# Rotary pieces of q and k kept in PSUM, in an attention and mixture-of-experts block on one core

## Chip, cores and metric

One core of one Trainium2 chip runs the whole kernel as one program. The metric is the time on the device in microseconds (us), the median over runs. A profiled execution of the same program gives the trace.

## The reference

The layer takes x of 16 batches x 1024 tokens x 256 channels in fp32. The part that matters here is how q and k are made:

```python
h  = _layernorm(x) * (1 + ca) + sa                 # modulation, one row per batch
xn = (h - mu) * rsqrt(var + eps) * gamma + beta    # second norm
q, k, v = heads(xn @ Wq + bq), heads(xn @ Wk + bk), heads(xn @ Wv + bv)   # 16 heads of 16
rot = stack([x1 * cos - x2 * sin, x1 * sin + x2 * cos])   # q and k; x1, x2: even and odd channels
```

After it come causal softmax attention, the output projection with residuals, and eight experts with gather and scatter-add.

## The kernel before

`build` runs five phases, each a block of five engine programs with a barrier between blocks. The change touches `phase1` alone. It makes q, k and v for all 16 batches and stores them to HBM; `phase2` (attention) reads them back.

**Pieces.** The q or k projection of 512 tokens is one piece. A batch has four (two blocks of 512 tokens, q and k), so there are 64 pieces, n = 0 to 63. A piece is two halves of 128 partitions x 512 columns: the even channels (e = 0) and the odd ones (e = 1) of all heads.

**Slots.** Each engine runs through the same numbered slots s; a batch is 8 slots, a piece two. What an engine does in a slot is written out in its `slot(s)`, and the lags between engines are fixed there by hand; semaphores order the rest. In steady state, with piece n at slots 2n, 2n+1 and so on:

- TensorE (PE): even slots `project(n)` at s = 2n (L658 to L668, two matmuls for each half, which the trace shows as eight records of L666); odd slots `values` for two token tiles (L670). After either, `turn_x` transposes normalized tiles of the next batch (L651), one or two in a slot.
- VectorE (DVE): odd slots `multiply(n)` at s = 2n+1: four scalar_tensor_tensor (L495), (projection + bias) x table, two into m1 with the cosines, two into m2 with the sines. Even slots first `take_rest(n)` at s = 2n+4 (L510), then `combine(n+1)` at the same slot (L504 m1 - m2, L505 m1 + m2, into qr). Around them stand the statistics: `take_x`, `take_h` (L445, L470), and once a batch `join_x`, `join_h`, `invert_x`, `invert_h` (L451, L475, L456 to L458, L481 to L483).
- ScalarE (ACT): `copy_x` (L567) takes transposed tiles from PSUM to x_t, `high(n)` (L584) rounds qr to bf16, `copy_v` (L576) takes the values from PSUM, `middle(n)` (L588) rounds what is left, then `first_norm` (L552) and `second_norm` (L559) of coming tiles. Once a batch each, a square root (L547) stands ahead of all this in its slot and waits for `join_x` or `join_h`.
- GpSimd (POOL): `modulate` (L628, L631) and `low(n)` (L635), which writes the third bf16 part.
- SyncE (SP): loads of x and stores of v, q and k by DMA, some 6.4 MB a batch.

**The banks of PSUM before.** Banks 0 and 1: transposed tiles, one bank for each of two tiles. Banks 2 to 5: the four halves of two pieces (q in 2, 3 and k in 4, 5). Banks 6 and 7: values, one bank for each of two tiles. `project(n)` waits until `multiply(n-2)` is done; `turn_x` and `values` wait for the copy of the tile two before.

In SBUF, m1, m2 and qr (two slots) hold the products and the rotated halves.

Of the kernel before, what the change touches and what calls it, by code (L numbers as in the profile page):

```python
# [17 lines left out]
F32 = mybir.dt.float32  # L18
# [306 lines left out]
def phase1(nc, x, ps, ident, cos_t, sin_t, w_all, bcol, rsx, nmx, mods_d, q_d, k_d, v_d):  # L325
# [5 lines left out]
    NP = 4  # L331
    STORES = 2 * 2 * NG
    RING = 3
    PS_X, PS_QK, PS_V = 0, 2, 6
    assert L == 2 * W and T == 2 * NP

    with ExitStack() as ctx:
# [13 lines left out]
        eps = sb("eps", [P, 1], F32)  # L351
        x_t = sb("x_t", [P, 2, KC, W], F32)
        m1 = sb("m1", [P, 2, W], F32)
        m2 = sb("m2", [P, 2, W], F32)
        qr = sb("qr", [P, 2, 2, W], F32)
        rest = sb("rest", [P, 2, 2, W], F32)
        stage = sb("stage", [P, 2, 3, 4, L], BF16)
        v_st = sb("v_st", [P, 2, NG, T, NV], F32)
# [18 lines left out]
        def parts(n, part):  # L377

            b, pr = n // NP, n % NP
            blk, which = pr // 2, pr % 2  # L380
            return stage[:, b % 2, part, 2 * which:2 * which + 2, blk * W:(blk + 1) * W]

        START = -23
        END = B * T + 6
# [52 lines left out]
        @block.vector  # L437
        def _(dve):
            def take_x(b, k):
                r = b % RING  # L440
                if k == 0:
                    dve.wait_ge(x_in[r], (b // RING + 1) * DMA)
                    reuse(dve, agx_done, b)
                for t in (2 * k, 2 * k + 1):
                    ins = dve.bn_stats(stx[:, t, :], xin[:, r, t, :])  # L445
                ins.then_inc(stx_done, 1)

            def join_x(b):
                dve.wait_ge(stx_done, 4 * b + 4)
                for t in range(T):  # L450
                    ins = dve.bn_aggr(agx[:, b % 2, t, :], stx[:, t, :])  # L451
                ins.then_inc(agx_done, 1)

            def invert_x(b):
                dve.wait_ge(sdx_done, b + 1)
                dve.reciprocal(rsx[:, b, :], sd[:, 0, :]).then_inc(rsx_done, 1)  # L456
                dve.wait_ge(rsx_done, b + 1)
                dve.scalar_tensor_tensor(nmx[:, b, :], agx[:, b % 2, :, 0], -1.0, rsx[:, b, :], ALU.mult, ALU.mult) \  # L458
                   .then_inc(statx, 1)

            def take_h(b, t):
                if t == 0:
                    reuse(dve, agh_done, b)
                if b == 0:
                    dve.wait_ge(h_mul, t + 1)
                    dve.tensor_tensor(h[:, 0, t, :], h[:, 0, t, :], mods[:, 0, M_SA, :], ALU.add).then_inc(first_done, 1)
                    dve.wait_ge(first_done, t + 1)
                else:
                    dve.wait_ge(h_done, (b - 1) * T + t + 1)
                dve.bn_stats(sth[:, t, :], h[:, b % 2, t, :]).then_inc(sth_done, 1)  # L470

            def join_h(b):
                dve.wait_ge(sth_done, b * T + T)
                for t in range(T):
                    ins = dve.bn_aggr(agh[:, b % 2, t, :], sth[:, t, :])  # L475
                ins.then_inc(agh_done, 1)

            def invert_h(b):
                p = b % 2
                dve.wait_ge(sdh_done, b + 1)  # L480
                dve.reciprocal(rsh[:, p, :], sd[:, 1, :]).then_inc(rsh_done, 1)  # L481
                dve.wait_ge(rsh_done, b + 1)
                dve.scalar_tensor_tensor(nmh[:, p, :], agh[:, p, :, 0], -1.0, rsh[:, p, :], ALU.mult, ALU.mult) \  # L483
                   .then_inc(stath, 1)

            def multiply(n):

                blk, which = n % NP // 2, n % 2
                dve.wait_ge(qk_done, n + 1)
                reuse(dve, rope_done, n)  # L490
                at = slice(blk * W, (blk + 1) * W)
                for m, table in ((m1, cos_t), (m2, sin_t)):
                    for e in range(2):
                        c = 2 * which + e
                        ins = dve.scalar_tensor_tensor(m[:, e, :], ps[:, PS_QK + c, :], bcol[:, c:c + 1], table[:, at],  # L495
                                                       ALU.add, ALU.mult)
                ins.then_inc(rope_mul, 1)

            def combine(n):

                s = n % 2
                dve.wait_ge(rope_mul, n + 1)
                reuse(dve, rest_done, n - 1)
                dve.tensor_tensor(qr[:, s, 0, :], m1[:, 0, :], m2[:, 1, :], ALU.subtract)  # L504
                dve.tensor_tensor(qr[:, s, 1, :], m1[:, 1, :], m2[:, 0, :], ALU.add).then_inc(rope_done, 1)  # L505

            def take_rest(n):
                dve.wait_ge(hi_done, n + 1)
                reuse(dve, lo_done, n - 1)
                dve.tensor_tensor(rest[:, n % 2], qr[:, n % 2], parts(n, 0), ALU.subtract).then_inc(rest_done, 1)  # L510

            def slot(s):
                n = (s - 1) // 2
                if s % 2 == 1 and 0 <= n < B * NP:
                    multiply(n)
                n = (s - 2) // 2
                if s % 2 == 0 and 0 <= n - 1 < B * NP:
                    take_rest(n - 1)
                if s % 2 == 0 and 0 <= n < B * NP:
                    combine(n)  # L520
                b, k = batch_at(s, 18)
                if b is not None and k == 0:
                    invert_x(b)
                b, k = batch_at(s, 6)
                if b is not None and k == 0:
                    invert_h(b)
                b, k = batch_at(s, 15)
                if b is not None:
                    take_h(b, k)
                    if k == T - 1:  # L530
                        join_h(b)
                b, k = batch_at(s, 23)
                if b is not None and k < 4:
                    take_x(b, k)
                    if k == 3:
                        join_x(b)

            dve.memset(eps[:, :], EPS)
            for s in range(START, END):
                slot(s)  # L540

        @block.scalar
        def _(act):
# [15 lines left out]
                nc.scalar.activation(h[:, p, t, :], h[:, p, t, :], ACT.Identity, bias=nmh[:, p, t:t + 1],  # L559
                                     scale=rsh[:, p, t:t + 1]).then_inc(xn_done, 1)  # L560

            def copy_x(b, t):
                act.wait_ge(xt_done, b * T + t + 1)
                blk, at = t // 4, t % 4
                if at == 0:
                    reuse(act, v_done, (b - 1) * T + 4 * blk + 4)
                nc.scalar.copy(x_t[:, blk, :, at * P:(at + 1) * P],  # L567
                               ps[:, PS_X + t % 2, 0:D].rearrange("p (k n) -> p k n", k=KC)).then_inc(xt_copied, 1)

            def copy_v(b, t):  # L570
                p = b % 2
                act.wait_ge(v_done, b * T + t + 1)
                if t == 0:
                    reuse(act, v_stored[p], b // 2 * (DMA * NG))
                dst = v_st[:, p, :, t, :].rearrange("p g (h n) -> p g h n", h=HG)[:, :, :, 0:D // HEADS]
                nc.scalar.copy(dst, ps[:, PS_V + t % 2, 0:D].rearrange("p (g h n) -> p g h n", g=NG, h=HG)) \  # L576
                  .then_inc(v_copied, 1)

            def high(n):
                act.wait_ge(rope_done, n + 1)  # L580
                b = n // NP
                if n % NP == 0:
                    reuse(act, stage_stored[b % 2], b // 2 * (DMA * STORES))
                nc.scalar.copy(parts(n, 0), qr[:, n % 2]).then_inc(hi_done, 1)  # L584

            def middle(n):
                act.wait_ge(rest_done, n + 1)
# [2 lines left out]
            def slot(s):  # L590
# [5 lines left out]
                    root(b, 1, agh, agh_done, sdh_done)  # L596
                for tiles, b in turned_in(s - 1):
                    for t in tiles:
                        copy_x(b, t)
                n = (s - 3) // 2  # L600
                if s % 2 == 1 and 0 <= n < B * NP:
                    high(n)
# [45 lines left out]

        @block.tensor
        def _(pe):  # L650
            def turn_x(b, t):  # L651
                pe.wait_ge(xn_done, b * T + t + 1)
                reuse(pe, xt_copied, b * T + t - 1)
                for k in range(KC):
                    ins = pe.transpose(ps[:, PS_X + t % 2, k * P:(k + 1) * P], h[:, b % 2, t, k * P:(k + 1) * P], ident[:, :])  # L655
                ins.then_inc(xt_done, 1)

            def project(n):  # L658

                b, blk, which = n // NP, n % NP // 2, n % 2  # L660
                pe.wait_ge(xt_copied, b * T + 4 * blk + 4)
                reuse(pe, rope_mul, n - 1)
                for e in range(2):
                    c = 2 * which + e
                    for k in range(KC):
                        ins = pe.matmul(ps[:, PS_QK + c, :], w_all[:, k, c * P:(c + 1) * P], x_t[:, blk, k, :],  # L666
                                        start=(k == 0), stop=(k == KC - 1))
                ins.then_inc(qk_done, 1)  # L668

            def values(b, t):  # L670
                reuse(pe, v_copied, b * T + t - 1)
                o = ps[:, PS_V + t % 2, 0:D]
                for k in range(KC):
                    ins = pe.matmul(o, x_t[:, t // 4, k, t % 4 * P:t % 4 * P + P], w_all[:, k, 2 * D:3 * D],  # L674
                                    start=(k == 0), stop=(k == KC - 1))
# [2 lines left out]
            def slot(s):  # L678
# [4 lines left out]
                        values(s // T, t)  # L683
                for tiles, b in turned_in(s):
                    for t in tiles:
                        turn_x(b, t)

            for s in range(START, B * T):
                slot(s)
# [934 lines left out]
```

## Time and profile before

| | |
|---|---|
| median of 3 runs | 3128.5 us (3128.36 to 3128.82) |
| the profiled execution's own time | 3130.67 us |
| its span, first to last instruction | 3128.6 us |
| mean granted TensorE clock over the span | 0.948 of full speed |
| phase 1, first projection to the last take_rest and low | about 93 to 621 us |
| phase 2, first matmul | after 640 us |
| DVE busy from 153.30 to 528.00 us | 365.62 of 374.70 us |
| PE, ACT, POOL busy in the same stretch | 279.14, 227.28, 290.74 us |

A row of a group of instructions reads: line, engine, operation, output and inputs by tile names, shape, count, then busy time in us and mean duration in ns of one, then the idle time of the engine ahead of them and what ended it. Two instructions of one engine overlap in their records by some 0.08 us, so durations add up to a little more than busy time. Busy time of a matmul is modelled, and a busy PE is not PE at its peak.

### The profile page before, as it was taken

To read this page: it belongs to the slowest core of one execution; us is meant where nothing else is said; L and a number is where in the kernel's file an instruction comes from. 1 tells how busy PE (TensorE), PEld (TensorE's weight loads), DVE (VectorE), ACT (ScalarE), POOL (GpSimd) and SP (SyncE) were. 2 spreads that over 40 slices of the span, in tenths; PEclk is the share of its full clock that TensorE was granted. 3 is DMA by queue.
4 is the path that set the end of the run, shared out by engine and by line. 5 is a ranking of instruction groups with operands and counts; after the bars stand their busy time and mean duration, and the time that the engine had idled before them with its cause. 6 is when DMAs were issued, how large, how long until landed. Compare 5 with 4: busy or idle time off the path is not lost. (4 is left out here: it accounts for less than half of the span.)

```text
span 3128.6 us, 48266 instructions
## 1 busy us (share of the span) xinstructions
PE 2768.8 (88%) x17467; PEld 1343.6 (43%) x17467; DVE 2213.2 (71%) x3164; ACT 1818.1 (58%) x3723; POOL 1060.7 (34%) x1294
## 2 busy tenths in 40 slices
PE   1677777669999999999999999999999889957997
PEld 0444444324444444444444444444444267744664
DVE  4999999867777777777777777777777245552221
ACT  1655656507777777777777777777777634421121
POOL 1787778421122111211122112212122166642231
PEclk7899899859999999999999999999999989988999
DMA  3366665663444454444444454445444087752342
GB/s 93 118 195 188 200 200 155 215 132 73 104 92 91 93 104 100 89 89 103 104 90 89 97 104 96 91 90 104 100 92 89 22 286 266 268 189 82 83 115 45
DMA packets 188549, 386.18 MB, mean 123 GB/s; under 512 B 33413, under 2 KB 104485, under 8 KB 175800
## 3 DMA queue, kind: packets, MB, share of 16 engines
q1 hardware_dynamic: 182170, 374.58, 46.7%
q0 software_dynamic: 6144, 8.52, 1.6%
q8 instruction: 141, 2.31, 0.3%
q14 instruction: 94, 0.77, 0.1%
HBM read 240.65 MB, written 144.53 MB: 123 GB/s over the span
## 5 line engine op out<-in xcount | busy, mean ns | idle before, releaser
L922 DVE TENSOR_REDUCE mx<-ps 128x2 f32<-128x1024 f32 (+3 forms) x1216 | 1371.6, 1167 | 397.7 <-PE ps L1010 302.4
L968 ACT ACTIVATE prob<-ps 128x512 f32<-128x512 f32 (+1 forms) x2560 | 1251.7, 560 | 539.8 <-PE ps L1028 531.0
L1003 PE MATMUL ps<-k_rows,q_rows 96*128 96x512 bf16 (+3 forms) x3072 | 910.9, 332 | 47.2 <-DMA k_rows<-k_parts 40.6
L1028 PE MATMUL ps<-q_rows,k_rows 99*128 99x512 bf16 (+3 forms) x3072 | 907.4, 329 | 14.2 <-ACT prob L968 5.8
L861 POOL TENSOR_SCALAR_AFFINE_SELECT prob<-prob 128x512 f32<-128x512 f32 x512 | 318.7, 634 | 1452.9 <-ACT prob L968 1452.9
L1047 PE MATMUL ps<-prob,v_rows 128*32 128x512 f32 (+3 forms) x6144 | 628.8, 497 | 0.0
L1028 PEld LDWEIGHTS ps<-q_rows,k_rows 99*128 99x128 bf16 x3072 | 273.1, 98 | 599.1 <-ACT prob L968 360.0
L1003 PEld LDWEIGHTS ps<-k_rows,q_rows 96*128 96x128 bf16 x3072 | 289.8, 98 | 277.7 <-DVE mx L922 60.8
L1010 PE MATMUL ps<-mask_b,unit_b 128*128 128x128 bf16 (+2 forms) x1408 | 348.6, 248 | 0.0
L666 PE MATMUL ps<-x_t,w_all 128*128 128x512 f32 x512 | 248.5, 631 | 0.0
L1047 PEld LDWEIGHTS ps<-prob,v_rows 128*32 128x32 f32 x6144 | 134.4, 108 | 246.1 <-ACT prob L968 123.3
L655 PE MATMUL ps<-ident,h 128*128 128x128 f32 x256 | 55.2, 317 | 151.2 <-ACT x_t L567 82.5
L628 POOL TENSOR_TENSOR h<-xin,mods_b 128x256 f32<-128x256 f32 x128 | 146.0, 1143 | 106.9 <-ACT xin L552 106.8
L635 POOL TENSOR_TENSOR stage<-rest,stage 128x1024 bf16<-128x1024 f32 x64 | 147.5, 2306 | 35.5 <-ACT stage L588 35.4
L1484 DVE SCALAR_TENSOR_TENSOR y<-ps,gx,gate 128x256 f32<-128x256 f32 x32 | 15.5, 484 | 195.9 <-PE ps L1575 195.9
L1010 PEld LDWEIGHTS ps<-mask_b,unit_b 128*128 128x128 bf16 x1408 | 139.5, 99 | 22.8
L1250 PE MATMUL ps<-wg,n_t 128*128 128x256 f32 x512 | 146.6, 409 | 0.0
L666 PEld LDWEIGHTS ps<-x_t,w_all 128*128 128x128 f32 x512 | 101.8, 207 | 104.1 <-issue 103.2
L1199 ACT COPY n_t<-ps 128x256 f32<-128x256 f32 x128 | 47.5, 371 | 155.2 <-PE ps L1238 155.2
L1177 DVE TENSOR_TENSOR x<-ps,res_b 128x256 f32<-128x256 f32 x128 | 54.4, 425 | 109.5 <-PE ps L1250 109.5
L674 PE MATMUL ps<-w_all,x_t 128*128 128x256 f32 x512 | 126.1, 390 | 3.3 <-ACT v_st L576 2.0
L1213 POOL TENSOR_TENSOR res_b<-res_b,a_b 128x256 f32<-128x256 f32 x128 | 93.0, 727 | 85.2 <-ACT res_b L1189 85.2
(154 smaller groups left out, 2777.6 us busy)
## 6 DMA issues: line engine op xcount, KB each, us to landing
k_rows<-k_parts SPq DMA_DIRECT2D x384, 128.0 KB, 7.3
v_ones<-v_st SPq DMA_DIRECT2D x64, 512.0 KB, 4.3
v_rows<-v_ones SPq DMA_DIRECT2D x64, 512.0 KB, 9.1
att<-o_sb SPq DMA_DIRECT2D x128, 256.0 KB, 2.5
att_b<-att SPq DMA_DIRECT2D x16, 2048.0 KB, 9.9
q_parts<-stage SPq DMA_DIRECT2D x128, 192.0 KB, 3.3
k_parts<-stage SPq DMA_DIRECT2D x128, 192.0 KB, 3.3
q_rows<-q_parts SPq DMA_DIRECT2D x64, 384.0 KB, 4.6
```

The source lines that it names most:

```text
L628: pool.tensor_tensor(h[:, p, t, :], xin[:, r, t, :], mods[:, r, M_CA1, :], ALU.mult).then_inc(h_mul, 1)
L635: pool.tensor_tensor(parts(n, 2), rest[:, n % 2], parts(n, 1), ALU.subtract).then_inc(lo_done, 1)
L666: ins = pe.matmul(ps[:, PS_QK + c, :], w_all[:, k, c * P:(c + 1) * P], x_t[:, blk, k, :], start=(k == 0), stop=(k == KC - 1))
L674: ins = pe.matmul(o, x_t[:, t // 4, k, t % 4 * P:t % 4 * P + P], w_all[:, k, 2 * D:3 * D], start=(k == 0), stop=(k == KC - 1))
L861: pool.affine_select(out=own, in_=own, compare_op=ALU.is_ge, fill=0.0, base=0, pattern=[[0, HG], [1, P]], channel_multiplier=-1).then_inc( ...
L922: dve.tensor_reduce(dst, src, AX.X, ALU.max).then_inc(a_free, 1)
L968: nc.scalar.activation(prob[:, (g * NPC + i) % RING, h, 0:w], src, ACT.Exp).then_inc(exp_done, 1)
L1003: ins = pe.matmul(ps[:, at, col:col + w], q[0:ROWS, g, h, i * P:(i + 1) * P], k[0:ROWS, g, h, k0:k0 + w], start=(r == 0), stop=True, skip_ ...
L1010: ins = pe.matmul(own, unit_b[:, :], mask_b[:, :].rearrange("p (o n) -> p o n", o=1) .to_broadcast([P, per, P]), start=False, stop=True, s ...
L1028: ins = pe.matmul(ps[:, PS_B + bank(g, n), at:at + w], k[0:AUG, g, h, j * P:(j + 1) * P], q[0:AUG, g, h, q0:q0 + w], start=True, stop=True)
L1047: ins = pe.matmul(ps[32 * h:32 * h + 32, PS_O, col:col + w], v[:, g, j, h, :], prob[:, (g * NPC + i) % RING, h, at:at + w], start=(j == 0) ...
L1250: ins = pe.matmul(o, n_t[:, r % 2, k, :], wg[:, p, k, :], start=False, stop=(k == KC - 1))
```

## The change

The two sine products are written back over the projection in PSUM, and `combine` writes the rotated halves there too; m2 and qr go. The halves of a piece now lie in two of six banks (2 to 7), in a ring of three pieces (`QR = 3`). The transposed tiles share bank 0 and the values share bank 1, two tiles in each bank, so `turn_x` and `values` wait until both tiles of the pair before are copied, and `copy_x` and `copy_v` until both tiles of their own pair are written. `project(n)` waits for `take_rest(n-3)` in place of `multiply(n-2)`. Nothing outside phase 1 changes.

```diff
-    PS_X, PS_QK, PS_V = 0, 2, 6
+    PS_X, PS_V, PS_QK, QR = 0, 1, 2, 3
...
-        m2 = sb("m2", [P, 2, W], F32)
-        qr = sb("qr", [P, 2, 2, W], F32)
...
+        def half(n, e):
+            return ps[:, PS_QK + n % QR * 2 + 1 - e, :]
+
+        def turned(n):
+            return ps[:, PS_QK + n % QR * 2:PS_QK + n % QR * 2 + 2, :]
...
-                for m, table in ((m1, cos_t), (m2, sin_t)):
-                    for e in range(2):
-                        c = 2 * which + e
-                        ins = dve.scalar_tensor_tensor(m[:, e, :], ps[:, PS_QK + c, :], bcol[:, c:c + 1], table[:, at],
-                                                       ALU.add, ALU.mult)
+                for e in range(2):
+                    c = 2 * which + e
+                    dve.scalar_tensor_tensor(m1[:, e, :], half(n, e), bcol[:, c:c + 1], cos_t[:, at], ALU.add, ALU.mult)
+                for e in range(2):
+                    c = 2 * which + e
+                    ins = dve.scalar_tensor_tensor(half(n, e), half(n, e), bcol[:, c:c + 1], sin_t[:, at], ALU.add, ALU.mult)
                 ins.then_inc(rope_mul, 1)
             def combine(n):
-                s = n % 2
                 dve.wait_ge(rope_mul, n + 1)
-                reuse(dve, rest_done, n - 1)
-                dve.tensor_tensor(qr[:, s, 0, :], m1[:, 0, :], m2[:, 1, :], ALU.subtract)
-                dve.tensor_tensor(qr[:, s, 1, :], m1[:, 1, :], m2[:, 0, :], ALU.add).then_inc(rope_done, 1)
+                dve.tensor_tensor(half(n, 1), m1[:, 0, :], half(n, 1), ALU.subtract)
+                dve.tensor_tensor(half(n, 0), m1[:, 1, :], half(n, 0), ALU.add).then_inc(rope_done, 1)
             def take_rest(n):
...
-                dve.tensor_tensor(rest[:, n % 2], qr[:, n % 2], parts(n, 0), ALU.subtract).then_inc(rest_done, 1)
+                dve.tensor_tensor(rest[:, n % 2], turned(n), parts(n, 0), ALU.subtract).then_inc(rest_done, 1)
...
-            def copy_x(b, t):
-                act.wait_ge(xt_done, b * T + t + 1)
+            def copy_x(b, t, last):
+                act.wait_ge(xt_done, b * T + last + 1)
...
             def copy_v(b, t):
-                act.wait_ge(v_done, b * T + t + 1)
+                act.wait_ge(v_done, b * T + t // 2 * 2 + 2)
...
-                nc.scalar.copy(parts(n, 0), qr[:, n % 2]).then_inc(hi_done, 1)
+                nc.scalar.copy(parts(n, 0), turned(n)).then_inc(hi_done, 1)
...
-            def turn_x(b, t):
+            def turn_x(b, t, first):
                 pe.wait_ge(xn_done, b * T + t + 1)
-                reuse(pe, xt_copied, b * T + t - 1)
+                reuse(pe, xt_copied, b * T + first)
...
             def project(n):
-                reuse(pe, rope_mul, n - 1)
+                reuse(pe, rest_done, n - QR + 1)
...
-                        ins = pe.matmul(ps[:, PS_QK + c, :], w_all[:, k, c * P:(c + 1) * P], x_t[:, blk, k, :],
+                        ins = pe.matmul(half(n, e), w_all[:, k, c * P:(c + 1) * P], x_t[:, blk, k, :],
...
             def values(b, t):
-                reuse(pe, v_copied, b * T + t - 1)
-                o = ps[:, PS_V + t % 2, 0:D]
+                reuse(pe, v_copied, b * T + t // 2 * 2)
+                o = ps[:, PS_V, t % 2 * D:t % 2 * D + D]
```

Here `first` and `last` are the first and last tile of the one or two that a slot turns.

## Rows read from the trace of the kernel before

**Rows 1.** The page's slices: busy tenths of each engine, 78.2 us each.

```profile
PE   1677777669999999999999999999999889957997
...
DVE  4999999867777777777777777777777245552221
...
POOL 1787778421122111211122112212122166642231
```

Columns of the next group: stretch and its length in us, busy us (x instructions) of PE, PEld, DVE, ACT and POOL, granted clock, DMA share, GB/s.

**Rows 2.** Busy time in 11 steady batches of phase 1.

```profile
153.30:528.00 374.70, 279.14 (x881) 158.12 (x880) 365.62 (x704) 227.28 (x464) 290.74 (x222) 0.90 0.61 190
```

**Rows 3.** Groups of DVE instructions by line and shape, 98 to 620 us.

```profile
L510 DVE TENSOR_TENSOR rest<-qr,stage 128x1024 f32<-128x1024 f32 x64 | 102.1, 1596 | 1.1 <-ACT stage L584 1.1
L495 DVE SCALAR_TENSOR_TENSOR m<-ps,bcol,sin_t 128x512 f32<-128x512 f32 x128 | 89.5, 741 | 0.0
L495 DVE SCALAR_TENSOR_TENSOR m<-ps,bcol,cos_t 128x512 f32<-128x512 f32 x128 | 88.9, 736 | 9.8 <-PE ps L666 9.1
L505 DVE TENSOR_TENSOR qr<-m 128x512 f32<-128x512 f32 x64 | 77.2, 1206 | 0.0
L504 DVE TENSOR_TENSOR qr<-m 128x512 f32<-128x512 f32 x64 | 63.7, 995 | 0.0
...
L483 DVE SCALAR_TENSOR_TENSOR nmh<-agh,rsh 128x8 f32<-128x8 f32 x15 | 12.5, 836 | 0.5
```

**Rows 4.** Single lines over the whole run: duration ns min/median/max.

```profile
L504 DVE TENSOR_TENSOR qr<-m x64: 678/1206/1218, 101.8 to 614.0; 128x512 f32<-128x512 f32 x64
L505 DVE TENSOR_TENSOR qr<-m x64: 676/1206/2609, 102.4 to 614.6; 128x512 f32<-128x512 f32 x64
L510 DVE TENSOR_TENSOR rest<-qr,stage x64: 1206/1484/2571, 108.2 to 616.4; 128x1024 f32<-128x1024 f32 x64
L495 DVE SCALAR_TENSOR_TENSOR m<-ps,bcol,sin_t x128: 734/742/745, 99.5 to 610.9; 128x512 f32<-128x512 f32 x128
L628 POOL TENSOR_TENSOR h<-xin,mods_b x128: 717/736/2666, 70.7 to 557.8; 128x256 f32<-128x256 f32 x128
L1439 DVE TENSOR_TENSOR same<-ps,idxf x8: 691/692/692, 2838.5 to 3077.9; 128x512 f32<-128x512 f32 x8
```

**Rows 5.** Timeline of DVE, 311 to 325 us: start, us.

```profile
313.45 1.21 DVE L504 TENSOR_TENSOR qr<-m 128x512 f32<-128x512 f32 x1
...
316.81 0.64 DVE L451 BATCH_NORM_AGGREGATE agx<-stx 128x2 f32<-128x6 f32 x8
...
321.44 0.68 DVE L504 TENSOR_TENSOR qr<-m 128x512 f32<-128x512 f32 x1
...
323.87 1.41 DVE L495 SCALAR_TENSOR_TENSOR m<-ps,bcol,cos_t 128x512 f32<-128x512 f32 x2 [0.20 <-PE ps L666]
```

**Rows 6.** Timeline of POOL over the same time.

```profile
312.41 1.70 POOL L628 TENSOR_TENSOR h<-xin,mods_b 128x256 f32<-128x256 f32 x1
...
320.91 2.40 POOL L628 TENSOR_TENSOR h<-xin,mods_b 128x256 f32<-128x256 f32 x1 [5.67 <-ACT xin L552]
```

**Rows 7.** Timeline of ACT and PE over the same time.

```profile
317.55 0.30 ACT L547 ACTIVATE sd<-agx,eps 128x8 f32<-128x8 f32 x1 [5.87 <-DVE agx L451]
317.76 0.63 ACT L567 COPY x_t<-ps 128x256 f32<-128x256 f32 x2
318.25 1.08 PE L655 MATMUL ps<-ident,h 128*128 128x128 f32 x4 [6.28 <-ACT x_t L567]
...
319.13 4.70 PE L666 MATMUL ps<-x_t,w_all 128*128 128x512 f32 x8
...
323.67 1.89 PE L674 MATMUL ps<-w_all,x_t 128*128 128x256 f32 x8
...
325.62 3.60 PE L666 MATMUL ps<-x_t,w_all 128*128 128x512 f32 x8
```

**Rows 8.** Busy time in the stretch with the lowered clock, columns as in rows 2.

```profile
314.50:321.30 6.80, 3.05 (x7) 1.91 (x8) 6.76 (x19) 3.75 (x9) 1.13 (x2) 0.50 0.93 246
```

**Rows 9.** All durations of the projection's matmuls, ns min/median/max.

```profile
L666 PE MATMUL ps<-x_t,w_all x512: 592/592/1062, 93.0 to 602.9; 128*128 128x512 f32 x171
```

More of the change, by code:

```diff
@@ L567, in copy_x @@
                 nc.scalar.copy(x_t[:, blk, :, at * P:(at + 1) * P],
-                               ps[:, PS_X + t % 2, 0:D].rearrange("p (k n) -> p k n", k=KC)).then_inc(xt_copied, 1)
+                               ps[:, PS_X, t % 2 * D:t % 2 * D + D].rearrange("p (k n) -> p k n", k=KC)).then_inc(xt_copied, 1)
             def copy_v(b, t):
                 p = b % 2
-                act.wait_ge(v_done, b * T + t + 1)
+                act.wait_ge(v_done, b * T + t // 2 * 2 + 2)
                 if t == 0:
@@ L575, in copy_v @@
                 dst = v_st[:, p, :, t, :].rearrange("p g (h n) -> p g h n", h=HG)[:, :, :, 0:D // HEADS]
-                nc.scalar.copy(dst, ps[:, PS_V + t % 2, 0:D].rearrange("p (g h n) -> p g h n", g=NG, h=HG)) \
+                nc.scalar.copy(dst, ps[:, PS_V, t % 2 * D:t % 2 * D + D].rearrange("p (g h n) -> p g h n", g=NG, h=HG)) \
                   .then_inc(v_copied, 1)
@@ L598, in slot @@
                     for t in tiles:
-                        copy_x(b, t)
+                        copy_x(b, t, tiles[-1])
                 n = (s - 3) // 2
@@ L650, in _ @@
         def _(pe):
-            def turn_x(b, t):
+            def turn_x(b, t, first):
                 pe.wait_ge(xn_done, b * T + t + 1)
-                reuse(pe, xt_copied, b * T + t - 1)
+                reuse(pe, xt_copied, b * T + first)
                 for k in range(KC):
-                    ins = pe.transpose(ps[:, PS_X + t % 2, k * P:(k + 1) * P], h[:, b % 2, t, k * P:(k + 1) * P], ident[:, :])
+                    ins = pe.transpose(ps[:, PS_X, t % 2 * D + k * P:t % 2 * D + (k + 1) * P], h[:, b % 2, t, k * P:(k + 1) * P], ident[:, :])
                 ins.then_inc(xt_done, 1)
@@ L685, in slot @@
                     for t in tiles:
-                        turn_x(b, t)
+                        turn_x(b, t, tiles[0])
             for s in range(START, B * T):
```

## The prediction

> **What bounds the kernel now.** I read the page's slices first, to place phase 1. In slices 2 to 6 DVE shows 9 and PE and POOL 7 or 8; two slices later PE takes over and stays at 9 [rows 1]. Phase 2 and what follows are not touched, so the question is what one batch costs in phase 1. The busy times by stretch say it plainly: from 153.30 to 528.00 us, 11 batches, DVE is busy 365.62 of 374.70 us, 98%; POOL 78%, PE 75%, ACT 61% [rows 2]. A batch takes 374.7 / 11 = 34.06 us, and DVE's instructions set it. Whatever comes off DVE comes off the time, until another chain is late.
>
> The groups of DVE instructions then show something odd [rows 3]. The two adds and subtracts of `combine` (L504, L505) have 512 columns like the four products of `multiply` (L495), yet take 995 and 1206 ns where a product takes 736 to 741. The single lines show the spread: the products hardly vary (734 to 745), while L504 runs from 678 to 1218, L505 from 676 to 2609 and L510 from 1206 to 2571 [rows 4]. So the shortest is the instruction's own cost, and the rest is a wait inside the record.
>
> The timelines say for whom. POOL's L628 starts at 312.41 and takes 1.70 us in place of its usual 0.736, ending at 314.11; DVE's L504 starts at 313.45 and ends at 314.66, that is 0.55 us after POOL's end: about its own time less the 0.08 by which records overlap. At 321.44, with L504 one of three DVE instructions in a row that got there first, L504 takes 0.68 and it is POOL that needs 2.40 us [rows 4 to 6]. The two engines take turns, an instruction at a time. The products, which read one tensor from PSUM and one from SBUF, never take part. What waits are DVE instructions with both tensors in SBUF.
>
> **What the change does on DVE.** After it, L504, L505 and L510 read one tensor from PSUM and one from SBUF. The nearest row for that is L1439, a tensor_tensor of 128x512 fp32 with one tensor in PSUM: 691 to 692 ns in all 8 instances, 14 ns over the shortest L504 [rows 4]. Per piece, on the means [rows 3]:
>
> - L504: 995 - 692 = 303 ns
> - L505: 1206 - 692 = 514 ns
> - L510: shortest 1206, plus 14 for its PSUM input, is 1220; 1596 - 1220 = 376 ns
>
> Sum 1193 ns, and times 64 pieces 76.4 us.
>
> What the trace does not show is a DVE instruction whose output is in PSUM, in the very bank that it reads. There are four of them a piece (two sine products, two of `combine`). Lower bound: nothing, 692 and 741 as they are. A bound for a mild fee is the difference between the two PSUM readers, 741 - 692 = 49 ns on each of the four, 0.2 us a piece, 12.5 us in all. The far bound is that reading and writing one bank halves the rate: 512 columns cost 1206 - 678 = 528 ns (L510 against L504, shortest each), so 2.1 us a piece. Against it speaks that a projection's second matmul of each half adds onto the bank that it writes, and all 512 records have a median of 592, equal to the minimum: accumulating costs no more than overwriting [rows 9]. I take nothing for the sum.
>
> One rule of the Trainium skill speaks against the change. In the rows, a PSUM input costs 14 ns (692 against 678) [rows 4]. "VectorE: DVE Perf Modes", section "The TRN2 errata", gives a fixed cost of 120 cycles for PSUM to SBUF against 58 for SBUF to SBUF at 0.96 GHz, 65 ns more; an estimate by it is 3 x 51 ns x 64 = 10 us less gain. The measured row disagrees in size, and I go by it.
>
> **The other engines.** ACT's `high` reads the same 1024 columns from PSUM instead of SBUF; ACT has 39% idle, and DVE meets its result one `multiply` later (at least 2.6 us, against 1.05 us of work). POOL loses its own waits. Dropping the wait of `combine` for `take_rest(n-1)` is worth nothing: they stand in that order on DVE anyway. SP's queue issues the same DMAs; their share rises from 0.61 to about 0.71 when a batch shrinks to 29 us, and 0.93 is seen in a stretch here [rows 2, 8].
>
> **The new waits.** `project(n)` now waits for `take_rest(n-3)`, slot 2n-2, for use by `multiply(n)` in slot 2n+1: between lie a combine, a multiply, a rest and a combine, some 6 us without statistics, against 3.6 us of matmuls and 1.9 of values. Fits. The shared banks matter where PE is already late. That is one place per batch: DVE ends `join_x` at 317.45 [rows 5], ACT's root waits for it, the copies of tiles 0 and 1 stand behind the root, PE's transposes of 2 and 3 wait for the copies, and the projection is behind them [rows 7]. It ends at 323.83 and DVE has waited 0.20 us for it [rows 5]. The transposes started at 318.25, after the first copy; now they need both, done at 318.39, so about 0.2 us later. DVE's own way from `join_x` to this multiply had nothing contended in it and stays some 6.3 us. So this stall, 9.1 us in all of phase 1 [rows 3], grows by 0.2 x 16 = 3 us at most, unless the clock changes. The clock: the granted clock is 0.50 from 314.5 to 321.3, after PE had been idle for most of 6.28 us, and that projection takes 4.70 us where the next takes 3.60 [rows 7, 8]. The idle time spans one rest and one combine of DVE, so it shrinks by 1.2 us or more, to 4 or 5. `turn_x` of tile 6 now stands behind ACT's other root, after `join_h`; from there DVE has a multiply, a rest and a combine (5.0 us at the new durations) and the statistics of two slots ahead of it, and PE's chain (root and copy 0.8, transposes 0.4, projection 3.6) is 4.8.
>
> At the end of phase 1 there are no statistics left, and a piece would cost DVE 2 x 736 + 2 x 741 + 2 x 692 + 1220 ns less seven overlaps of 0.08, 5.0 us [rows 3, 4]; PE alone needs 3.60 + 1.89 us [rows 7]. That caps the gain of the last four or so; I take 2 us off.
>
> **Sum.** 76.4 - 3 - 2 = 71.4 us. Against the profiled execution, 3130.7 - 71.4 = 3059.3; the median of the runs stands 2.2 us below it, so 3057.
>
> **Rivals.**
>
> *PE's late chain takes a part back.* If the clock is lowered over the whole projection behind `join_x`, it takes up to 7.2 us instead of 3.6, and the chain is 0.8 + 0.2 + 0.9 + 7.2 = 9.1 us against DVE's 6.4: a stall of 2.7 in place of 0.5 now, 2.2 x 11 steady batches = 24 us. Time 3081. For it: PE has less slack in a batch of 29 us (25.4 busy) [rows 2]. Against: less idle, and the clock was low over only part of the projection [rows 7].
>
> *In-place in PSUM is slow* (the other side). At 528 ns more on each of four instructions, 2.11 us a piece x 64 = 135 us against 76 saved: 3128.5 + 59 + 5 = about 3192. It decides from 76.4 / 256 = 0.30 us on each. Against it: the accumulating matmuls [rows 9].
>
> *The waits inside the records are not for a second SBUF input*, but for whatever POOL does, and stay. Then only 14 ns x 3 x 64 = 2.7 us and the 3 us of stall are added: 3134, within 0.2% (6.3 us, about what a measurement of this kernel tells from no change). Against it: the products' 734 to 745, with POOL 78% busy [rows 2, 4]. The Trainium skill, "SBUF — State Buffer", section "Who interferes with whom", has DVE instructions with at most one SBUF input not contending with GpSimd; by that rule the forecast stands, and the products agree.
>
> *More is saved*: L483, two SBUF inputs and 836 ns [rows 3], waits less, and the 9.1 us of PE stalls go: down to about 3043.
>
> **Numbers.** Forecast 0.62, PE's chain 0.20, slow in place 0.08, contention stays 0.05, all else 0.05. The range reaches from the best case, 3042, to 3095, which holds PE's chain with the 12.5 us of a mild fee: about 8 in 10. Faster 0.87, same 0.05, slower 0.08.
>
> **What the profile after would show.** L504 and L505's successors at a flat 0.69 us and the rest at 1.22, with no spread; the in-place products at 0.74; POOL's L628 and L631 near 0.73, but for the small instructions. Steady batches of about 29 us, with DVE still over 95% busy. PE's idle time ahead of the transposes at 4 or 5 us. If DVE's share falls below 90% in those batches, PE's chain has taken over; if the in-place products stand over 1.0 us, the second rival is true.

## The result, and the profile after

The changed kernel takes 3057.0 us (median of 4 runs, 3055.5 to 3058.2) against 3128.7 us: a ratio of 0.976, with a 95% interval of 0.975 to 0.978. The forecast was 3057. That the two agree to the microsecond is in part luck: a cost of 13.9 us was missed, and several smaller terms came out better than forecast by about as much.

The groups of DVE instructions after the change, 90 to 560 us, answer to [rows 3]. `multiply` is now L499 (cosine) and L502 (sine), `combine` L509 and L510, `take_rest` L515, and the small last instructions of `invert_x` and `invert_h` are L463 and L488:

```profile
L502 DVE SCALAR_TENSOR_TENSOR ps<-ps,bcol,sin_t 128x512 f32<-128x512 f32 x128 | 90.0, 748 | 0.0
L499 DVE SCALAR_TENSOR_TENSOR m<-ps,bcol,cos_t 128x512 f32<-128x512 f32 x128 | 88.7, 734 | 7.0 <-PE ps L671 6.7
L515 DVE TENSOR_TENSOR rest<-ps,stage 128x1024 f32<-128x1024 f32 x64 | 77.2, 1207 | 1.1 <-ACT stage L589 1.1
...
L510 DVE TENSOR_TENSOR ps<-m,ps 128x512 f32<-128x512 f32 x64 | 44.1, 689 | 0.0
L509 DVE TENSOR_TENSOR ps<-m,ps 128x512 f32<-128x512 f32 x64 | 43.8, 684 | 0.0
...
L463 DVE SCALAR_TENSOR_TENSOR nmx<-agx,rsx 128x8 f32<-128x8 f32 x14 | 22.2, 1588 | 0.5
L488 DVE SCALAR_TENSOR_TENSOR nmh<-agh,rsh 128x8 f32<-128x8 f32 x15 | 10.7, 714 | 0.5
```

The single lines (duration ns min/median/max) answer to [rows 4]. The spread of the three rope groups is gone, and so is that of POOL's `modulate`:

```profile
L509 DVE TENSOR_TENSOR ps<-m,ps x64: 678/685/690, 103.2 to 543.8; 128x512 f32<-128x512 f32 x64
...
L510 DVE TENSOR_TENSOR ps<-m,ps x64: 682/689/695, 103.8 to 544.4; 128x512 f32<-128x512 f32 x64
...
L515 DVE TENSOR_TENSOR rest<-ps,stage x64: 1200/1206/1226, 109.3 to 546.1; 128x1024 f32<-128x1024 f32 x64
...
L633 POOL TENSOR_TENSOR h<-xin,mods_b x128: 716/729/903, 71.3 to 496.3; 128x256 f32<-128x256 f32 x128
...
L463 DVE SCALAR_TENSOR_TENSOR nmx<-agx,rsx x16: 166/1666/1678, 70.4 to 469.4; 128x8 f32<-128x8 f32 x16
```

`low` still runs as often as before, but of the 64 L509 the 22 that start while it runs take 683 ns on the mean, like all others.

The last line is what the prediction had not reckoned with: an instruction of eight columns that takes 1.67 us. The same line in the kernel before, in the same view:

```profile
L458 DVE SCALAR_TENSOR_TENSOR nmx<-agx,rsx x16: 166/461/540, 69.7 to 526.4; 128x8 f32<-128x8 f32 x16
```

On the timelines of the changed kernel it starts at 293.71 and ends with POOL's `low` (L640), which runs to 295.37. In 13 of 16 batches it starts while `low` runs, and each time it ends some 0.02 us after it:

```profile
293.71 1.67 DVE L463 SCALAR_TENSOR_TENSOR nmx<-agx,rsx 128x8 f32<-128x8 f32 x1
```

```profile
293.24 2.13 POOL L640 TENSOR_TENSOR stage<-rest,stage 128x1024 bf16<-128x1024 f32 x1
```

The same 11 batches by stretch (columns as in [rows 2]) take 321.5 us instead of 374.7, 29.2 us a batch, with DVE busy 99%:

```profile
149.80:471.30 321.50, 269.22 (x873) 156.43 (x872) 318.73 (x705) 226.34 (x463) 217.79 (x221) 0.93 0.71 223
```

Where the time came from, as differences in DVE's busy and idle time in phase 1:

| | before, us | after, us | difference |
|---|---|---|---|
| the three rope groups, 64 x the sum of their means | 243.0 | 165.1 | -77.9 |
| small instruction of `invert_x`, 14 instances | 6.5 | 22.2 | +15.7 |
| small instruction of `invert_h`, 15 instances | 12.5 | 10.7 | -1.8 |
| idle ahead of the cosine products | 9.8 | 7.0 | -2.8 |
| sine and cosine products, and idle ahead of `take_h` | | | -1 |
| sum | | | about -68 |

Phase 2's first matmul comes 70.9 us earlier (647.2 to 576.3 us), 3 us more than the table gives. Some 2 us of them are overlap of the records: an instruction that has waited overlaps the next one by less (L505 by 0.067 us on the mean, its successor L510 by 0.081), so durations understate what a wait costs. The last 2 us of the 73.0 by which the profiled span shrinks (3128.6 to 3055.6) lie in later phases.

### The profile page after: what moved, and what is told of

It is laid out like the page before. It is cut to its first block and busy times, and to the rows that moved or that the text cites. A ratio compares the mean times of both kernels' runs of the same rounds, so it can differ in the third digit from the quotient of the medians.

```text
span 3055.6 us, 48203 instructions
## 1 busy us (share of the span) xinstructions
PE 2754.5 (90%) x17467; PEld 1341.3 (44%) x17467; DVE 2146.6 (70%) x3164; ACT 1816.3 (59%) x3723; POOL 967.6 (32%) x1294
## 5 line engine op out<-in xcount | busy, mean ns | idle before, releaser
L640 POOL TENSOR_TENSOR stage<-rest,stage 128x1024 bf16<-128x1024 f32 x64 | 136.4, 2132 | 30.1 <-ACT stage L593 30.1
L633 POOL TENSOR_TENSOR h<-xin,mods_b 128x256 f32<-128x256 f32 x128 | 93.7, 734 | 133.9 <-ACT xin L557 133.9
```

Source lines behind the costliest of these rows:

```text
L640: pool.tensor_tensor(parts(n, 2), rest[:, n % 2], parts(n, 1), ALU.subtract).then_inc(lo_done, 1)
```

## The experiments

Twelve kernels ran. Each was timed in turn with the kernel before on one chip; a ratio is to that kernel. The medians of the kernel before in the three sets were 3130.0, 3130.3 and 3132.1 us.

### The change taken apart: which input matters

**sine_in_sbuf.** Sine products in SBUF again, rotated halves in PSUM:

```diff
-    ins = dve.scalar_tensor_tensor(half(n, e), half(n, e), bcol[:, c:c + 1], sin_t[:, at], ...)
+    ins = dve.scalar_tensor_tensor(m2[:, e, :], half(n, e), bcol[:, c:c + 1], sin_t[:, at], ...)
...
-    dve.tensor_tensor(half(n, 1), m1[:, 0, :], half(n, 1), ALU.subtract)
-    dve.tensor_tensor(half(n, 0), m1[:, 1, :], half(n, 0), ALU.add).then_inc(rope_done, 1)
+    dve.tensor_tensor(half(n, 1), m1[:, 0, :], m2[:, 1, :], ALU.subtract)
+    dve.tensor_tensor(half(n, 0), m1[:, 1, :], m2[:, 0, :], ALU.add).then_inc(rope_done, 1)
```

> The changed kernel with the sine products in SBUF again (m2); the rotated halves still go to PSUM. The two tensor_tensor of combine then have both inputs in SBUF, the rest has not. If the waits inside the records come from a second SBUF input: combine's two go back from 0.68 and 0.69 us to about 1.0 and 1.2 us, the rest stays at 1.21, and the time is 3057 + 64 x 0.83 = about 3105 us, or a few us more if PE's chain adds. If they come from something else that the change did: combine stays at 0.69 and the time at 3057.

Measured 3103.0 us, ratio 0.991 (0.990 to 0.993). Groups of DVE instructions:

```profile
L516 DVE TENSOR_TENSOR rest<-ps,stage 128x1024 f32<-128x1024 f32 x64 | 77.1, 1205 | 1.1 <-ACT stage L590 1.1
L511 DVE TENSOR_TENSOR ps<-m 128x512 f32<-128x512 f32 x64 | 62.1, 970 | 0.0
L510 DVE TENSOR_TENSOR ps<-m 128x512 f32<-128x512 f32 x64 | 57.5, 899 | 0.0
...
L489 DVE SCALAR_TENSOR_TENSOR nmh<-agh,rsh 128x8 f32<-128x8 f32 x15 | 23.5, 1564 | 0.5
```

`combine` contends again, though it writes to PSUM, and the rest does not: the second SBUF input decides, instruction by instruction. The time was forecast well, the split was not: `combine` gave back 31.7 us, not 53, and `invert_h`'s small instruction another 12.8 (10.7 to 23.5). Here part of the wait went to another two-input instruction.

**halves_in_sbuf.** The other half: sine products in PSUM, `combine` writes to qr in SBUF.

```diff
+    reuse(dve, rest_done, n - 1)
-    dve.tensor_tensor(half(n, 1), m1[:, 0, :], half(n, 1), ALU.subtract)
-    dve.tensor_tensor(half(n, 0), m1[:, 1, :], half(n, 0), ALU.add).then_inc(rope_done, 1)
+    dve.tensor_tensor(qr[:, n % 2, 0, :], m1[:, 0, :], half(n, 1), ALU.subtract)
+    dve.tensor_tensor(qr[:, n % 2, 1, :], m1[:, 1, :], half(n, 0), ALU.add).then_inc(rope_done, 1)
...
-    dve.tensor_tensor(rest[:, n % 2], turned(n), parts(n, 0), ALU.subtract).then_inc(rest_done, 1)
+    dve.tensor_tensor(rest[:, n % 2], qr[:, n % 2], parts(n, 0), ALU.subtract).then_inc(rest_done, 1)
```

> The changed kernel with the rotated halves in SBUF again (qr); the sine products still go to PSUM. Now combine has one input in SBUF and an output in SBUF, and the rest has both inputs in SBUF. Second-input theory: combine stays at 0.69 us, the rest goes from 1.21 to about 1.6, time 3057 + 64 x 0.39 = about 3082 us. If an output in PSUM had a price of its own, combine would get shorter than 0.684 and 0.689 by it; I expect at most 0.01 us. Rival: all of the gain hangs on combine, and the rest stays at 1.21 since POOL is less in the way: 3057 to 3060.

Measured 3084.5 us, ratio 0.986 (0.984 to 0.987). Single lines of `combine`, then groups:

```profile
L511 DVE TENSOR_TENSOR qr<-m,ps x64: 668/674/681, 103.1 to 569.2; 128x512 f32<-128x512 f32 x64
...
L512 DVE TENSOR_TENSOR qr<-m,ps x64: 672/674/683, 103.7 to 569.8; 128x512 f32<-128x512 f32 x64
...
L517 DVE TENSOR_TENSOR rest<-qr,stage 128x1024 f32<-128x1024 f32 x64 | 100.6, 1572 | 1.1 <-ACT stage L591 1.1
...
L500 DVE SCALAR_TENSOR_TENSOR m<-ps,bcol,cos_t 128x512 f32<-128x512 f32 x128 | 88.9, 735 | 20.7 <-PE ps L673 20.1
...
L489 DVE SCALAR_TENSOR_TENSOR nmh<-agh,rsh 128x8 f32<-128x8 f32 x15 | 17.4, 1161 | 0.5
```

This gives the disputed price by itself: with the output in SBUF `combine` takes 674 and 674 ns, with the output in the bank that it reads 685 and 689. In place in PSUM costs 11 to 15 ns, against the 300 ns from which that rival would have decided. The rest contends again at 1572: 23.4 us, where the forecast for it was 25. That the time too came out within 3 us of the forecast is luck: `invert_x`'s small instruction fell from 22.2 to 2.7 us, `invert_h`'s grew by 6.7, and 13.7 us went into waiting for PE.

**low_as_memset.** The other side of the contention, in the kernel before:

```diff
-    pool.tensor_tensor(parts(n, 2), rest[:, n % 2], parts(n, 1), ALU.subtract).then_inc(lo_done, 1)
+    pool.memset(parts(n, 2), 0.0).then_inc(lo_done, 1)
```

> The kernel before, with POOL's low replaced by a memset of its output (the third bf16 part is left out, zeros are stored): POOL is still busy in its place but reads no SBUF there, for some 0.9 us instead of 2.13. If DVE's two-input instructions wait for POOL's instructions that read SBUF: L504, L505 and L510 lose the part of their waits that low causes, about half of 1.19 us a piece, so time about 3090 us (3075 to 3105), and no L505 of 2.6 us is left. If the waits had another source: L504, L505, L510 keep their means of 995, 1206 and 1596 and the time is 3128.

Measured 3076.0 us, ratio 0.983 (0.981 to 0.985), at the fast end. Groups of DVE instructions, then DVE's and POOL's timelines:

```profile
L510 DVE TENSOR_TENSOR rest<-qr,stage 128x1024 f32<-128x1024 f32 x64 | 89.7, 1401 | 1.1 <-ACT stage L584 1.1
...
L504 DVE TENSOR_TENSOR qr<-m 128x512 f32<-128x512 f32 x64 | 63.6, 995 | 0.0
...
L505 DVE TENSOR_TENSOR qr<-m 128x512 f32<-128x512 f32 x64 | 44.6, 697 | 0.0
```

```profile
309.82 1.21 DVE L504 TENSOR_TENSOR qr<-m 128x512 f32<-128x512 f32 x1
310.96 0.68 DVE L505 TENSOR_TENSOR qr<-m 128x512 f32<-128x512 f32 x1
```

```profile
308.89 1.59 POOL L631 TENSOR_TENSOR h<-h,mods_b 128x256 f32<-128x256 f32 x1
310.43 0.95 POOL L635 MEMSET stage<- 128x1024 bf16 x1
```

L505 falls from 1206 to 697, L504 keeps 995. They had met different partners. Before, L504 started in `low` once and did not wait for it; L505 started in it 11 times, for 2.43 us on the mean, and these are 19 of its 34 us of waits. The rest of L505's gain and the unchanged mean of L504 come from other meetings with `modulate`, as the schedule shifted. L505 here runs 310.96 to 311.64 across a memset of 310.43 to 311.38 and doesn't wait; nor do any of the 23 that start in a memset (676 to 679 ns). So not any work of POOL holds DVE's two-input instructions, but work that reads SBUF. The Trainium skill, "SBUF — State Buffer", section "Who interferes with whom", says so too: two SBUF inputs on DVE contend only with GpSimd instructions that read SBUF. This trace agrees.

### The ring and the shared banks

**ring_of_two.** Four banks for pieces, two each for tiles and values. Not shown here: the waits for tiles and values are those of before again.

```diff
-    PS_X, PS_V, PS_QK, QR = 0, 1, 2, 3
+    PS_X, PS_QK, PS_V, QR = 0, 2, 6, 2
```

> The changed kernel with four banks for the pieces (a ring of two) and two banks each for transposed tiles and values, with the waits of before for these. project(n) must then wait for take_rest(n-2), which stands in slot 2n on DVE, one combine and one set of statistics ahead of multiply(n). By that DVE waits for most of a projection of 3.6 us at every piece: 3.6 less 1.2 (combine) less 0.4 to 1.0 (statistics) = 1.4 to 2.0 us x 64 = 90 to 130 us, time 3147 to 3187, slower than the kernel before. If the third piece is not needed: 3057 or less, since the banks are no longer shared.

Measured 3200.4 us, ratio 1.023 (1.021 to 1.024), slower than before and 13 us beyond my bracket. The single line of the cosine products and two rows of PE's timeline:

```profile
L499 DVE SCALAR_TENSOR_TENSOR m<-ps,bcol,cos_t x128: 729/744/753, 99.0 to 682.6; 128x512 f32<-128x512 f32 x128
its engine sat idle before it (us, times) until:
  PE ps L671: 148.8, 63
```

```profile
308.37 3.67 PE L671 MATMUL ps<-x_t,w_all 128*128 128x512 f32 x8 [1.77 <-DVE rest L515]
...
316.41 3.67 PE L671 MATMUL ps<-x_t,w_all 128*128 128x512 f32 x8 [2.42 <-DVE rest L515]
```

DVE waits 148.8 us for projections that wait for the rest: 63 times, 2.4 us each. With the halves kept in PSUM for longer the third pair of banks is not a refinement but what the gain hangs on.

**shared_banks_alone.** The kernel before, with `PS_X, PS_V, PS_QK = 0, 1, 2` and the changed kernel's waits for tiles and values, and nothing else.

> The kernel before with nothing but the shared banks: transposed tiles in one bank, values in one, with the stricter waits; products and halves stay in SBUF. My forecast charged 0.2 us a batch, 3 us in all: 3132. If the shared banks are free: 3128.5. If they are dear (PE held at each pair): over 3135.

Measured 3146.0 us, ratio 1.0053 (1.0039 to 1.0067): five times what I charged. Groups of DVE instructions, against [rows 3], and the worst projection on PE's timeline:

```profile
L510 DVE TENSOR_TENSOR rest<-qr,stage 128x1024 f32<-128x1024 f32 x64 | 106.4, 1663 | 1.1 <-ACT stage L584 1.1
...
L495 DVE SCALAR_TENSOR_TENSOR m<-ps,bcol,cos_t 128x512 f32<-128x512 f32 x128 | 88.9, 736 | 16.3 <-PE ps L666 15.7
L505 DVE TENSOR_TENSOR qr<-m 128x512 f32<-128x512 f32 x64 | 79.0, 1235 | 0.0
L504 DVE TENSOR_TENSOR qr<-m 128x512 f32<-128x512 f32 x64 | 69.8, 1091 | 0.0
```

```profile
286.08 1.09 PE L655 MATMUL ps<-ident,h 128*128 128x128 f32 x4 [5.06 <-ACT x_t L567]
286.96 6.13 PE L666 MATMUL ps<-x_t,w_all 128*128 128x512 f32 x8
```

6.5 us are idle time ahead of the products (16.3 against 9.8), as in the projection of 6.13 us, most of it at the lower clock (the granted clock of that stretch is 0.58 on the mean). Another 12 us are longer records of L504, L505 and L510.

**shared_copies_first** and **before_copies_first.** The same, and the kernel before, with `copy_x` ahead of the two roots in ACT's slot:

```diff
+    for tiles, b in turned_in(s - 1):
+        for t in tiles:
+            copy_x(b, t)
     b, k = batch_at(s, 19)
     if b is not None and k == 0:
         root(b, 0, agx, agx_done, sdx_done)
...
-    for tiles, b in turned_in(s - 1):
-        for t in tiles:
-            copy_x(b, t)
```

> The kernel before with the shared banks and with copy_x ahead of the roots. The shared banks alone cost 15.6 us, of which the trace shows 6.5 as DVE idle time ahead of the cosine products and about 11 as longer waits inside the combine's and rest's records. If both come from PE and ACT being held behind join_x, this takes most of the 15.6 back: 3130 to 3135. If the price is a shift against POOL that copies cannot mend: 3140 or more.

> The kernel before with copy_x ahead of the roots, nothing else. DVE's idle time ahead of the cosine products falls from 9.8 to about 4 us; what the contended instructions do is open, since they meet POOL in other places: 3123 if nothing moves there, 3115 to 3135 with it. If the 13 us that the same edit gave in the changed kernel were PE's chain, it should give as much here.

Measured 3130.5 us (ratio 0.9994, 0.9985 to 1.0003) and 3130.1 us (0.9995, 0.9986 to 1.0004). With the copies out from behind the root, shared banks cost nothing: their price is the place behind `join_x`, both parts of it. By itself the edit brings nothing before the change. The cause is on view in the groups of before_copies_first:

```profile
L510 DVE TENSOR_TENSOR rest<-qr,stage 128x1024 f32<-128x1024 f32 x64 | 109.5, 1710 | 1.1 <-ACT stage L584 1.1
...
L495 DVE SCALAR_TENSOR_TENSOR m<-ps,bcol,cos_t 128x512 f32<-128x512 f32 x128 | 88.6, 732 | 4.4 <-PE ps L666 3.8
L505 DVE TENSOR_TENSOR qr<-m 128x512 f32<-128x512 f32 x64 | 82.9, 1295 | 0.0
...
L483 DVE SCALAR_TENSOR_TENSOR nmh<-agh,rsh 128x8 f32<-128x8 f32 x15 | 8.1, 537 | 0.5
```

Idle time falls by 5.4 us and L483 by 4.4, and the rest and L505 grow by 7.4 and 5.7: POOL is met in other places.

### What the change left on the table

**copies_first.** The same edit in the changed kernel.

> The changed kernel with copy_x ahead of the two square roots in ACT's slot. PE's transposes then no longer wait for join_x, and the projection behind them is done before DVE wants it. DVE's idle time ahead of the cosine products, 7.0 us in phase 1, loses all but the first (3.6) and the last four pieces (1.9): gain 1 to 3 us, 3054 to 3056. If PE's chain is what holds the batch at 29.2 us, as the rival of the late chain has it: more than 10 us less.

Measured 3043.6 us, ratio 0.972 (0.971 to 0.973), 13.4 us less than the changed kernel. Groups of DVE instructions:

```profile
L499 DVE SCALAR_TENSOR_TENSOR m<-ps,bcol,cos_t 128x512 f32<-128x512 f32 x128 | 88.7, 733 | 4.7 <-PE ps L671 4.3
...
L463 DVE SCALAR_TENSOR_TENSOR nmx<-agx,rsx 128x8 f32<-128x8 f32 x14 | 15.1, 1076 | 0.5
L488 DVE SCALAR_TENSOR_TENSOR nmh<-agh,rsh 128x8 f32<-128x8 f32 x15 | 7.1, 475 | 0.5
```

Taken alone, "more than 10 us" was my sign that PE's chain holds the batch. The trace says otherwise: idle time falls by 2.3 us only, the two small instructions by 7.1 and 3.6. The edit moved ACT and with it POOL, and the small instructions met `low` later in its course: L463 still starts in it in 13 batches, but with 1.09 us of it left on the mean, where it was 1.65. A time alone would have confirmed the wrong theory.

**invert_early.** `invert_x` and `invert_h` ahead of the rest and `combine` in DVE's slot:

```diff
+    b, k = batch_at(s, 18)
+    if b is not None and k == 0:
+        invert_x(b)
+    b, k = batch_at(s, 6)
+    if b is not None and k == 0:
+        invert_h(b)
     n = (s - 2) // 2
     if s % 2 == 0 and 0 <= n - 1 < B * NP:
         take_rest(n - 1)
```

> The changed kernel with invert_x and invert_h ahead of take_rest and combine in DVE's slot, so that the small two-input instruction of invert_x meets POOL idle and not in low. That instruction (8 columns) takes 1588 ns on the mean after the change against 461 before; it should fall to about 0.4 us: 1.1 us x 14 = 16 us of DVE time. But it stands between join_x and the multiply that PE's chain is late for, where the slack is 0.04 to 0.85 us a batch: so I expect only 0.5 us a batch to arrive, 3057 - 6 = 3051, and the DVE idle time ahead of the cosine products to grow by some 8 us. If PE's chain does not matter: 3041. If the wait only moves to another instruction: 3057.

Measured 3045.5 us, ratio 0.973 (0.971 to 0.974), 11.5 us less.

```profile
L499 DVE SCALAR_TENSOR_TENSOR m<-ps,bcol,cos_t 128x512 f32<-128x512 f32 x128 | 89.0, 736 | 20.9 <-PE ps L671 20.2
...
L488 DVE SCALAR_TENSOR_TENSOR nmh<-agh,rsh 128x8 f32<-128x8 f32 x15 | 4.9, 325 | 0.5
...
L463 DVE SCALAR_TENSOR_TENSOR nmx<-agx,rsx 128x8 f32<-128x8 f32 x14 | 2.7, 193 | 0.5
```

25.3 us come off the two small instructions and 13.9 go into waiting for PE: the chain behind `join_x` is next in line, as expected, with all sizes larger than I wrote.

**after_low_memset.** The changed kernel with `low` as a memset, edit as above.

> The changed kernel with POOL's low as a memset (the third bf16 part is left out, zeros are stored). If nothing of the rope instructions contends any more, the three rope groups keep 0.684, 0.689 and 1.207 us and only the two small two-input instructions get shorter: invert_x's from 1588 to under 500 ns (it stood behind low), 15 us less on DVE. PE's chain behind join_x then takes most of it back, as it did when the inverts were moved (13.9 of 25.3): time 3057 less 3 to 10, and DVE idle ahead of the cosine products above 12 us. If the rope instructions still waited for POOL: they fall too, and the time by more than 15 us.

Measured 3045.8 us, ratio 0.972 (0.971 to 0.973). The small instruction falls from a median of 1666 to 168 ns, with the rope instructions unmoved (0.683, 0.686, 1.206 us) and 20.7 us idle ahead of the cosine products:

```profile
L463 DVE SCALAR_TENSOR_TENSOR nmx<-agx,rsx x16: 166/168/539, 70.2 to 457.4; 128x8 f32<-128x8 f32 x16
```

```profile
L499 DVE SCALAR_TENSOR_TENSOR m<-ps,bcol,cos_t 128x512 f32<-128x512 f32 x128 | 88.9, 736 | 20.7 <-PE ps L671 20.5
```

So it was `low` that it stood behind. The gain of 11.2 us is a little over the 3 to 10 I expected.

**both_moved.** Both moves. **copies_invx.** Copies first, and only `invert_x` moved.

> Both moves at once: copies ahead of the roots, inverts ahead of the rests. With PE's chain out of the way the whole 16 us of invert_x arrive, and the 1 to 3 us of stalls: 3057 - 18 = 3039 (3036 to 3043). If the two gains only add as measured alone (6 and 2): 3049.

> The changed kernel with copies ahead of the roots and only invert_x ahead of the rest; invert_h stays behind combine. In the trace with both moved, invert_x's small instruction takes 548 ns and invert_h's 757; with the copies alone it is 1076 and 475. Taking the better of each: 15 x 0.28 = 4 us less than both moved, 3034. If the small instruction meets POOL elsewhere once the batch is shorter: 3038 as before.

Measured 3038.3 us (0.9705, 0.9691 to 0.9718) and 3035.4 us (0.9694, 0.9681 to 0.9708). The second is the fastest kernel here, 22 us ahead of the changed one, though not clear of the first. DVE's groups in it:

```profile
L499 DVE SCALAR_TENSOR_TENSOR m<-ps,bcol,cos_t 128x512 f32<-128x512 f32 x128 | 88.7, 733 | 4.9 <-PE ps L671 4.4
...
L463 DVE SCALAR_TENSOR_TENSOR nmx<-agx,rsx 128x8 f32<-128x8 f32 x14 | 7.7, 548 | 0.5
L488 DVE SCALAR_TENSOR_TENSOR nmh<-agh,rsh 128x8 f32<-128x8 f32 x15 | 7.5, 500 | 0.5
```

## Why the prediction was right, and where it was not

- **DVE is the bound.** Right; it is busy 99% of the steady stretch after.
- **The waits inside the records, 303 + 514 + 376 = 1193 ns a piece.** Right: 1217 ns measured. halves_in_sbuf put the rest's part back (23.4 of 25 us), sine_in_sbuf some 60% of `combine`'s (31.7 of 53), and low_as_memset took some away from POOL's side.
- **A PSUM input at 14 ns, an output in place at nothing.** The input costs nothing to be seen (674 ns against 678 for the shortest with both in SBUF), the output 11 to 15 ns. The Trainium skill, "VectorE: DVE Perf Modes", section "The TRN2 errata", gives 120 fixed cycles for a PSUM source against 58, by estimate 65 ns more at its 0.96 GHz. These durations do not show them, and the 10 us that the prediction worked out from them would have been wrong.
- **The small instructions, put at nothing.** The missed term. I named `invert_h` (L483) as something that might wait less, and wrote that DVE's way from `join_x` to the multiply behind it had nothing contended in it and would stay at some 6.3 us. `invert_x`'s instruction lies on that way. It has two SBUF inputs, and it waited already, for `modulate`, 0.46 us in place of 0.17. Now it arrives while `low` runs: +15.7 us, a fifth of the gain. The way was 6.22 us in the steady batches before and is 7.33 to 7.41 after. The instruction on DVE's timeline before, in the batch that the prediction read:

```profile
322.88 0.46 DVE L458 SCALAR_TENSOR_TENSOR nmx<-agx,rsx 128x8 f32<-128x8 f32 x1
```

- **The stall behind `join_x`, +3 us.** Its change came out as -4.5 us, but not because PE's chain was any less late. Of the 9.1 us that I took for this stall 3.3 are the wait for the very first projection; 5.8 are the stall. After the change 1.3 us of stall are left, since DVE comes to that multiply 1.1 us later and PE is ready: the missed wait hides the stall. Take the wait away, as after_low_memset does, and the way is 5.91 us and DVE stands 0.7 to 2.1 us in each steady batch, 14.2 us in eleven. With a way of 6.22 us, as before, that would be 10.8 us against 5.8, an estimate that leaves out what else the memset moves. By it 0.2 us a batch was too little. In the kernel before, the shared banks alone cost 15.6 us, most of it as longer waits of instructions that no longer contend here. I argued this term from one batch's timeline, with the rest of the schedule held still.
- **Why the total fits all the same.** 13.9 us of waits were missed. Against them stand 7.5 us at the stall, 1.5 at the three rope groups, some 2 of overlap, 1.4 less idle ahead of `take_h` and 2 in later phases. The first is mostly the missed wait's own doing. The others are terms that the prediction had a little low or did not have, and that they add up to this is chance.
- **PE idle 4 or 5 us ahead of the transposes.** About 4.27 in every steady batch. The last pieces are bound by PE: 1.9 us ahead of four of them, 2 charged.
- **The rivals.** In place in PSUM is slow: refuted. Contention stays: refuted. PE's chain takes a part back: not to be seen in the changed kernel (7.0 us idle, of which 3.6 are the very first piece), but only because `invert_x`'s wait covers it. It is the next bound: invert_early, after_low_memset and halves_in_sbuf show 20.7 to 20.9 us as soon as DVE gets shorter behind `join_x`. More is saved: L483 gave 1.8 us, and most of the stall went, but L458's successor took more than both.

What stays open: 1 us or so that neither the table nor the overlaps place. Why the slots of shared_banks_alone meet POOL for longer was not followed instruction by instruction. The price of the shared banks in the changed kernel could not be measured by itself, as six banks for pieces leave only two for the rest.

## What to carry to other kernels

Where two engines take turns on something, compare an instruction's shortest with its mean: the difference can be a wait that no idle column shows. Here it was won by moving one operand to PSUM, without any less work. Then list every instruction left that still contends, the small ones too, and ask what each will meet once the schedule moves; here eight columns took 1.67 us, more than the 1.21 of the rest with its 1024. A wait on the path to a late partner hides that partner's lateness, so taking it away gives less than its length (11.2 us of 26.8 in after_low_memset). Read the trace of each experiment, not only its time: copies_first gave the number that the wrong theory had asked for.

## What the runs showed of the hardware that was not expected

- A DVE instruction with 8 columns and two SBUF inputs waits out a GpSimd instruction of 2.13 us: median 1666 ns, against 168 when that GpSimd instruction only writes.
- A GpSimd memset of 0.95 us, over which such a DVE instruction runs, leaves it at 0.68 us.
- A DVE tensor_tensor that reads and writes one PSUM bank runs at full rate: 685 to 689 ns for 512 columns, against 674 with its output in SBUF.
